# First transfers of a mixture-of-experts kernel put in another order, and four register loads put in a row

## The reference, cut to what matters

```python
def _L0_cond_ref(x, subjects, weights, bias):      # x (64, 64, 512), weights (8, 64, 64)
    w = weights[subjects]
    b = bias[subjects]
    out = jnp.einsum('bct,bcd->bdt', x, w)
    return out + b[:, :, None]

def _L0_ffn_ref(hidden_states, ...):               # rows of 512, 4096 of them
    x = hidden_states.reshape(-1, H)
    w, sel = _route(x, gate_weight, expert_bias)   # 4 of 16 experts by grouped sigmoid scores
    out = _moe(x, w, sel, gate_proj, up_proj, down_proj)
    shared = jax.nn.silu(x @ shared_gate.T) * (x @ shared_up.T) @ shared_down.T
    return (out + shared).reshape(B, S, H)

x = x + _L0_ffn_ref(_L0_cond_ref(x, itok_B_0_7, L0_cond_weights, fside_8xS_0), ...)
```

## Time and profile before

| | us |
|---|---|
| median of 3 runs | 835.27 |
| lowest and highest run | 833.45 and 836.64 |
| the profiled execution's own time | 834.17 |
| span of the profiled execution | 832.4 |
| TensorE busy in the span | 818.8 (98%) |
| VectorE, ScalarE, GpSimd busy | 486.7, 391.4, 433.9 |

### The profile page before, as it was taken

How to read it: one execution, slowest core, us unless ns; L and a number is a source line. 1 busy time by engine, 2 the same in 40 slices (tenths; PEclk the granted TensorE clock), 3 DMA queues, 4 the chain that set the end, 5 groups by cost and what they waited for, 6 DMA issues and landing times.

```text
span 832.4 us, 19356 instructions
## 1 busy us (share of the span) xinstructions
PE 818.8 (98%) x4136; PEld 654.5 (79%) x4137; DVE 486.7 (58%) x986; ACT 391.4 (47%) x815; POOL 433.9 (52%) x400
## 2 busy tenths in 40 slices
PE   9999999999999999999999999999999999999995
PEld 5578878787888888888888888888888887887884
DVE  5788877635554546744457446647557466464541
ACT  4864467545333335533345334545455354443341
POOL 5503111436466666467565666465475674766334
PEclk9999999999999999999999999999999999999998
DMA  8986966799999999899998999799998999998755
GB/s 290 398 317 184 236 176 180 175 251 260 217 267 190 199 189 189 182 275 245 194 189 167 293 232 207 185 274 207 237 266 187 282 257 220 243 196 177 151 64 78
DMA packets 145305, 181.52 MB, mean 218 GB/s; under 512 B 30570, under 2 KB 103922, under 8 KB 142834
## 3 DMA queue, kind: packets, MB, share of 16 engines
q0 software_dynamic: 37776, 89.08, 52.6%
q1 hardware_dynamic: 106528, 80.45, 36.4%
q10 hardware_dynamic: 834, 10.49, 3.4%
HBM read 82.52 MB, written 67.17 MB: 180 GB/s over the span
## 4 chain that ended last, share of the span: by engine, by line
PE 91%; ACT 2%; DMA 2%; issue 2%; DVE 2%; DVEq 0%; POOLq 0%; POOL 0%; ACTq 0%; SPq 0%
PE psGU L1087 46%; PE psY L1087 23%; PE psY L1145 4%; PE psH L964 4%; PE psGU L1128 3%; PE psGU L1129 3%; PE psGU L1130 3%; DMA raw_w<-ffn_w 1%; PE psT L964 1%; PE psM L1115 1%; PE psGU L1013 1%; ACT x_ring L910 1%; PE psY L1013 0%; DMA x_ring<-x_pairs 0%; PE psH L990 0%
## 5 line engine op out<-in xcount | busy, mean ns | idle before, releaser
L1087 PE MATMUL psGU<-split_w,xT_pair 128*128 x1716 | 416.2, 391 | 0.6 <-DVE xT_pair L1594 0.4
L1087 PEld LDWEIGHTS psGU<-split_w,xT_pair 128*128 128x128 f32 x1716 | 321.9, 188 | 71.9 <-issue 2.3
L675 POOL DMA_INDIRECT out<-y_ring,idx_all x143 | 229.8, 1607 | 206.7 <-SPq L562 189.9
L923 ACT ACTIVATE aT<-psGU 128x256 f32<-128x256 f32 x143 | 54.9, 384 | 336.3 <-PE psGU L1087 336.3
L1087 PE MATMUL psY<-split_w,hidT_hi 128*128 x572 | 190.6, 414 | 0.2 <-issue 0.2
L670 POOL DMA_INDIRECT tok_ring<-h_rows,idx_all x143 | 148.7, 1040 | 70.7 <-issue 42.7
L1675 DVE SCALAR_TENSOR_TENSOR aT<-aT,w_ring,psGU 128x256 f32<-128x256 f32 x143 | 66.9, 468 | 162.9 <-ACT aT L923 162.3
L1594 DVE TENSOR_TENSOR xT_pair<-psT,xT_pair 128x512 fp32r<-128x512 f32 x143 | 98.8, 691 | 70.3 <-ACT xT_pair L736 50.7
L819 ACT ACTIVATE y_ring<-psY 128x512 f32<-128x512 f32 x173 | 104.2, 604 | 29.4 <-PE psY L1145 27.1
L1087 PE MATMUL psY<-split_w,hidT_lo 128*128 x286 | 113.0, 395 | 0.0
L1087 PEld LDWEIGHTS psY<-split_w,hidT_hi 128*128 128x128 f32 x572 | 96.9, 189 | 14.1 <-issue 0.5
(11 more groups left out here) (237 smaller groups left out, 670.5 us busy)
## 6 DMA issues: line engine op xcount, KB each, us to landing
x_ring<-tok_ring SPq DMA_DIRECT2D x284, 128.0 KB
raw_w<-ffn_w SPq DMA_DIRECT2D x17, 1536.0 KB, 9.5
out<-y_ring POOLq DMA_DIRECT2D x32, 256.0 KB, 10.9
x_ring<-x_pairs SPq DMA_DIRECT2D x12, 512.0 KB, 8.6
h_rows<-tok_ring SPq DMA_DIRECT2D x16, 256.0 KB, 9.6
h_rows<-y_ring SPq DMA_DIRECT2D x16, 256.0 KB, 9.7
tok_ring<-h_rows,idx_all POOLq DMA_INDIRECT x143, 6.4
out<-y_ring,idx_all POOLq DMA_INDIRECT x143, 6.3
```

Source lines behind the costliest of these rows:

```text
L675: pool.indirect_dma_start(out[:, :], bass.IndirectOffsetOnAxis(idx_all[:, r:r + 1], 0), y_ring[:, r % YRING, :], None, compute_op=ALU.add) ...
L923: act.activation(silu[:, t.slot % 2, :], psGU[t.slot % 2][:, 0:I], ACT.Silu).then_inc(silu_ready, 1)
L1087: mm = pe.matmul(dst, a[:, slot, c], w(at + col + k * H), start=(k == 0 and a is high and at == 0), stop=(k == parts - 1 and a is low))
```

## The change

SyncE issues `itok_row` first, ahead of `cond_sb`, `itok8` and `fside2`. ScalarE no longer issues it, starts with the x pairs 0 and 1 one behind the other, and waits for `cond_sb` ahead of pair 2 instead of pair 1. GpSimd reads the four subject numbers of step 0 into registers in one go, ahead of its wait for `cond_sb`; before, it read two, made two copies, and read two more.

```diff
         def _(sp):
 
+            sp.dma_start(itok_row[:], itok.unsqueeze(0)).then_inc(itok_loaded, 16)
             sp.dma_start(cond_sb[:], cond_w).then_inc(cond_loaded, 16)
             sp.dma_start(itok8[:], itok.partition_broadcast(NS)).then_inc(fside_loaded, 16)
             sp.dma_start(fside2[:], fside).then_inc(fside_loaded, 16)
@@
             pool.wait_ge(itok_loaded, 16)
 
+            def subject_column(b):
+
+                return (pool.value_load(itok_row[0:1, b:b + 1]) & (NS - 1)) * C
+
+            first_columns = {b: subject_column(b) for b in (0, 1, 3, 2)}
             word = None
@@
                     if m == 0:
-                        columns = [(pool.value_load(itok_row[0:1, b:b + 1]) & (NS - 1)) * C for b in (first, second)]
+                        columns = [first_columns[b] for b in (first, second)]
@@
         def _(act):
-            act.dma_start(itok_row[:], itok.unsqueeze(0)).then_inc(itok_loaded, 16)
             for m in range(X_PAIRS):
-                if m == 1:
+                if m == 2:
                     act.wait_ge(cond_loaded, 16)
                 load_pair(act, m)
```

## The result

| | before | changed |
|---|---|---|
| median of 22 runs each, us | 836.99 | 840.64 |
| lowest and highest | 833.45, 841.35 | 836.84, 845.74 |
| profiled execution, own time | 834.17 | 842.55 |
| its span | 832.4 | 840.8 |

The ratio is 1.0043, with a 95% interval of 1.0026 to 1.006: slower by 2.2 to 5.0 us. I had forecast +2.2 from the median of the three runs then shown, and the medians are 3.65 apart; the median over all 22 of before is itself 1.7 higher than that of the three. The result lies outside the range given (833.8 to 839.6). The two profiled executions are 8.4 us apart, more than the medians, so the first task is to see which of those 8.4 us belong to the change.

A forecast was written before the change was run, and what follows sets the result against it. TensorE, busy for 98% of the span, was taken as the bound, so a late `cond(2)` shifts the end: 6.28 - 4.12 = +2.2 us on the median 835.27 gives 837.4, range 833.8 to 839.6.

The forecast's parts named there:

- T - 4.12: Start of the kernel: shift of `cond(2)`, from its start at T + 5.35 against 9.47 before; forecast +2.2 us.
- T: Landing time of the `cond_sb` load: 3.61 us before the change, forecast 6.28 after it.
- The late weights: Start: `cond_sb` lands behind x pairs 0 and 1, delaying `cond(2)` and so the kernel by 2.2 us.
- Order of issue: DMA at the start: a transfer starts when the one issued earlier on the other queue is nearly through; +2.2 us.
- The rule of taking turns: Rival, chance 0.15: DMA engines alternate between queues packet by packet, `cond_sb` lands at 4.8, shift +0.7 us.
- my first rival: Start: `cond_sb` gets in front of x pair 1 and lands at 4.97, shift +0.85 us; chance 0.20.
- the main case: Start: x pair 1 goes in front of `cond_sb`, which lands at 6.28, shift +2.2 us; chance 0.45.
- the branch that I had left to the range: VectorE at the start: `subj1h` waiting for `fside2` costs 0.3 us if `fside2` keeps landing 1.3 us after `cond_sb`.
- The register loads: GpSimd at the start: loads ahead of the `cond_sb` wait cost nothing, and copies without the gap win 0.43 us.
- The clock rival: TensorE after warm-up: a 1.9 us standstill undoes the clock rise, costing 1.5 to 3.0 us more; chance 0.10.
- So whatever time the start wins or loses ... is handed on: TensorE is busy from 8.5 to 25 us, so a shift of `cond(2)` passes on to the kernel's end.
- No gain to be had: Start: with `cond_sb` still landing at 3.61, the change could win at most 0.5 us.

The follow-up runs named there:

- e9: The changed kernel with one empty semaphore increment added on ScalarE behind the x loads: 837.39 us, ratio 1.0032 to the kernel before.
- e12: The changed kernel itself, unaltered, measured a third time on another chip beside new runs of the kernel before: 839.41 us against 834.81, ratio 1.0067.
- e3: The kernel before with pair 1 issued ahead of the `cond_sb` wait and register loads in a row, `itok_row` staying on ScalarE: ratio 0.9993.

## Why the prediction was wrong, point by point

The step that failed is "I take the shift of `cond(2)` as the change of the kernel's time", with that shift counted at full speed (T - 4.12). The late weights were to cost 2.2 us and cost 1.15 to 1.3 at `cond(2)`; half speed added up to 2.7 there, and a stall at the end of ScalarE's program, which the sum did not have, makes the end 2.0 to 3.4 us longer in the traces. That +2.2 is no further from the measured +3.65 is luck: its one term was too large by 1.0, and two others were not in it. Another 1.7 us of the miss come from the median of three runs that I started from; with the later median the same sum gives 839.2. (The range's upper end, by its own terms 835.27 + 2.9 + 1.2, is 839.4 and not 839.6, which changes nothing here.)

- **Order of issue** held. From 2.4 to 3.6 the changed kernel moved pair 0, then the weights, then pair 1 (queues, packets, MB, share, in 2.4:3.6, 3.7:4.3 and 4.3:5.4; ScalarE's queue is q10):

```profile
q10 hardware_dynamic: 106, 0.43, 87.4%
q1 hardware_dynamic: 1, 0.00, 0.4%
...
q1 hardware_dynamic: 110, 0.23, 96.2%
q10 hardware_dynamic: 15, 0.02, 10.8%
...
q10 hardware_dynamic: 107, 0.44, 97.5%
q1 hardware_dynamic: 34, 0.02, 6.8%
```

  Of the last 34 packets of q1, 11 are the rest of the weights and the others small. The rule of taking turns, which the Trainium skill has in DMA: Bandwidth & Descriptors, Queues, rings and completion order, would have mixed them in each window; this trace disagrees. But the tie went the other way: `itok_row` took SyncE 0.36 us, not 0.54, so `cond_sb` went out at 1.23, a few hundredths ahead of pair 1. It was my first rival (T = 4.97), not the main case (6.28), and T was 5.27.
- **The shift T - 4.12** held where the speed was full: in the third trace, T was about 5.34 (first copy at 5.60), which gives `cond(2)` at 10.69; it came at 10.77. What set it there was the branch that I had left to the range: `fside2` landed at 6.48, and the clearing behind `subj1h` ended just ahead of the bias copy.
- **The register loads**, which were to cost nothing ahead of T and to win 0.43, held: 13 copies in 3.81 us from 5.53 on, without the gap of the earlier trace rows.
- **The clock rival** failed by its chance, 0.10, and by being left out of the range. Its price, 1.5 to 3.0 us, was right (2.74 in the profiled execution). I argued from the end of the program that a pause does not lower the clock at once. But the clock did not have to fall: in the changed kernel it had not risen yet when the warm-up ended. In the table, the seven traces with a pause of at most 0.41 us reach full speed between 4.1 and 7.3. The four with the changed kernel's start (pauses of 0.71 to 0.93) reach it at 5.5, 5.6, 13.3 and 14.0, and the three others with a pause of 0.76 or more at 11.2, 12.2 and 16.4. So a pause goes with a late rise in five of seven traces, and what decides in a single execution is not shown. The Trainium skill, TensorE: Matmul & The Clock Gate, Part 1, says that the same kernel warms up at different points in different runs; three traces of this one agree (full speed from 13.3, 5.5 and 5.6 us).
- **"So whatever time the start wins or loses ... is handed on"** failed by what it left out. It is handed on (3.9 us at `cond(2)`, 3.7 at the first routed tile, 192.4 against 196.1), but the change also takes one instruction out of ScalarE's program, which I costed as a DMA issue and nothing else. That put a wait of 5.66 us ahead of ScalarE's last two copies and made the end 3.2 us longer in the trace; on the median it is 2.0, by the two sets of runs of e9 and e12.
- **No gain to be had** held: e3, the change without its harmful part, is at 0.9993. The 0.5 us that I allowed didn't come, because pair 1 landed no earlier (7.30 against 7.37).

So the sum should have been the late weights (+1.2 at `cond(2)`), the clock (0 to +2.7, some +2 in the median on one chip) and ScalarE's end (+2); the first is the only one that I counted. They come to more than the 3.65 measured, since the clock's part differs from one execution to the next; on the third chip, where the change cost 4.6, they fit.

## What to carry to other kernels

When several queues are filled at the start, list the issues of all of them by time: the transfer that the first chain needs goes out first, and a tiny load behind large ones lands as late as they do. A warm-up of TensorE should reach the first real matmul; whoever delays that matmul has to look at it again (12 in place of 8 took 2.2 us off here). Before a change of a few microseconds is put down to what it moves, look at the last 10 us of the trace too, because one instruction more or less on an engine can move a stall there; an empty instruction tells.

## What the runs showed that I had not expected

- An empty instruction on ScalarE shortens the end of one kernel by 2 to 3 us (9.3 us against 11.4 to 12.4; 2.0 on the median) and is worth nothing in the other.
- Pair 1 landed at 7.37, 7.30 and 7.0, whether issued at 3.63 or at 1.81. What holds it up is open.
- Passes at half speed stand under a granted clock of 1.00 in the windows of the first 13 us, because the record begins with the rise.
- Full speed began anywhere from 5.5 to 14.0 us in four traces with the same start, and at 4.1 to 7.3 in seven with next to no pause.
- Seven of eight traces with SyncE's new order took longer over the routed stage than all six with the old one, by 0.1 to 3.3 us. Why is open.
- The same change measured 1.0043, 1.0101 and 1.0067 in three measurements, with the intervals of the first two apart.
